# Reordering every engine's list of steps in a fused layer kernel, so that fp32r matmuls stand in fewer groups

## What is computed

```python
h = _L0_tok_ref(...)                    # S4D: K = 2 Re sum_n Cc[c,h,n] exp(dtA[h,n] * l), l < 1024
h = concat([cls_tok, h], axis=1)        # 129 rows of 64 steps
h = h + attn(layernorm(h))              # 1024 -> 128, gelu, two passes of one hydra block, 128 -> 1024
h = h + ffn(layernorm(h))               # 1024 -> 1024, plus a routed low-rank term of 8 experts

def hydra(u):                           # d 128, inner 256, 4 heads, state 16, conv of 7 taps
    z, xBC, dt = split(u @ in_w.T)
    dt = softplus(dt + dt_bias)         # forward and backward
    xs, B, C = split(silu(causal_conv(xBC)))
    y = scan forward + scan backward, shifted by one step, + xs * (xs @ fcD_w.T + D)
    yz = y * silu(z)
    return (yz * rsqrt(mean(yz**2) + 1e-5) * norm_w) @ out_w.T

def ffn(x):
    logits = x @ router_W.T + router_b  # 15; softmax, top 8, mapped to experts
    return x @ base_W.T + base_b + 2 * ((x @ A.T) * w) @ B
```

## Time and profile before

| | |
|---|---|
| median of 3 runs | 2334.94 us (2334.63 to 2346.7) |
| profiled execution | 2339.94 us, span 2338.2 us |
| PE busy | 2161.3 us, 92% of the span |
| DVE busy | 1847.3 us, 79% |
| ACT busy | 1528.2 us, 65% |
| POOL busy | 1091.2 us, 47% |
| mean granted clock | 0.968 |
| DMA | 132.61 MB, mean 57 GB/s |

### The profile page before, as it was taken

One profiled execution on the slowest core, in us unless ns is written; L12 is line 12 of the kernel. 1 busy time (PEld: TensorE's weight loads), 2 busy tenths in 40 slices (PEclk: granted clock), 3 DMA queues, 4 the chain that ended last, 5 costly groups with the idle time before them and its releaser, 6 DMA issues.

```text
span 2338.2 us, 51899 instructions
## 1 busy us (share of the span) xinstructions
PE 2161.3 (92%) x14117; PEld 1805.6 (77%) x14117; DVE 1847.3 (79%) x4980; ACT 1528.2 (65%) x2921; POOL 1091.2 (47%) x1350
## 2 busy tenths in 40 slices
PE   1356799999999999999999999999999999999998
PEld 1245688888888888888888888888888888888776
DVE  6847688888888888888888888888888888888764
ACT  2546576766677766667666767666777666676652
POOL 2534355444455444455444554444554444554331
PEclk9756799999999999999999999999999999999999
DMA  4400122112222122221122221122211222211211
GB/s 92 117 29 24 35 64 64 42 54 63 63 63 61 35 61 63 63 63 48 47 63 63 63 63 40 55 63 63 63 58 36 63 63 63 63 47 47 69 39 33
DMA packets 90061, 132.61 MB, mean 57 GB/s; under 512 B 20379, under 2 KB 63559, under 8 KB 90006
## 3 DMA queue, kind: packets, MB, share of 16 engines
q1 hardware_dynamic: 79176, 125.60, 18.2%
q10 hardware_dynamic: 10830, 6.35, 1.1%
HBM read 55.17 MB, written 76.74 MB: 56 GB/s over the span
## 4 chain that ended last, share of the span: by engine, by line
issue 43%; PE 27%; POOL 9%; DVE 7%; ACT 6%; POOLq 1%; DVEq 0%; ACTq 0%; DMA 0%; SPq 0%
PE bank L1611 5%; PE bank L1512 5%; POOL CB L901 4%; PE bank L1567 3%; PE bank L1542 2%; DVE NF L1241 2%; ACT L1006 2%; POOL XD L852 2%; PE bank L1685 1%; PE bank L1669 1%; POOL RS L886 1%; PE bank L1544 1%; PE bank L1543 1%; POOL RS L865 1%; PE bank L1659 1%
## 5 line engine op out<-in xcount | busy, mean ns | idle before, releaser
L1512 PE MATMUL bank<-w_hi,XHI 128*128 128x512 f32 (+1 forms) x1560 | 622.9, 399 | 0.0
L1512 PE MATMUL bank<-w_lo,XHI 128*128 128x512 f32 (+1 forms) x1560 | 554.7, 356 | 0.0
L1512 PE MATMUL bank<-w_hi,XLO 128*128 128x512 f32 (+1 forms) x1560 | 554.4, 355 | 0.0
L1147 DVE SCALAR_TENSOR_TENSOR CX<-bank,cw,CX 128x252 f32<-128x252 f32 (+5 forms) x804 | 335.7, 460 | 61.8 <-ACT CX L944 61.6
L901 POOL TENSOR_TENSOR CB<-CB,CM 48x252 f32<-48x252 f32 (+5 forms) x402 | 292.7, 728 | 153.6 <-ACT CM L929 142.7
L1512 PEld LDWEIGHTS bank<-w_hi,XLO 128*128 128x128 f32 x1560 | 295.5, 189 | 46.9
L1512 PEld LDWEIGHTS bank<-w_lo,XHI 128*128 128x128 f32 x1560 | 296.8, 190 | 41.4
L1512 PEld LDWEIGHTS bank<-w_hi,XHI 128*128 128x128 f32 x1560 | 296.4, 190 | 41.2
L929 ACT ACTIVATE T<-bank 64x512 f32<-64x512 f32 x256 | 151.4, 592 | 261.1 <-PE bank L1601 256.5
L865 POOL TENSOR_TENSOR RS<-VE,half_neg 128x1 f32<-128x1 f32 x65 | 35.5, 546 | 369.9 <-DVE VE L1339 369.9
L892 POOL TENSOR_TENSOR RB<-m_gt,AS 128x512 fp32r<-128x512 f32 x134 | 164.9, 1231 | 56.8 <-DVE AS L1413 56.8
(11 more groups left out here) (295 smaller groups left out, 5332.5 us busy)
## 6 DMA issues: line engine op xcount, KB each, us to landing
carried<-T SPq DMA_DIRECT2D x65, 512.0 KB, 4.8
T<-carried SPq DMA_DIRECT2D x65, 512.0 KB, 3.9
out<-HB SPq DMA_DIRECT2D x129, 256.0 KB, 3.2
tables<-tab SPq DMA_DIRECT2D x8, 560.0 KB, 4.3
TB<-tables SPq DMA_DIRECT2D x64, 70.0 KB, 2.7
carried<-U SPq DMA_DIRECT2D x65, 64.0 KB, 3.6
XM<-carried SPq DMA_DIRECT2D x65, 64.0 KB, 4.8
XI<-in_x SPq DMA_DIRECT2D x128, 32.0 KB, 2.8
```

Of the source, the lines that this page charges most:

```text
L1147: inc(STT(CX[:, c, :, s:CS], src[:, :, 0:CS - s], cw[:, c, k:k + 1], CX[:, c, :, s:CS], ALU.mult, ALU.add), "conv")
L1512: ins = mm(bank[:, 0:c1 - c0], xs_[:, 1 - p, k, :], ws[:, k, c0:c1], start=(c0 == HID and k == 0 and n == 0), stop=(last == k and n == 2))
```

## The change

Only the order of calls at the end of the `body` functions of POOL, ACT, DVE and PE. No step is added or taken away, no wait and no operand is changed, and SP's list is the same. The core of the diff (of DVE's list, 76 lines long, the two parts that are spoken of):

```diff
@@ GpSimd @@
+                    kernel_q()
                     swap()
-                    kernel_q()
...
                     add_bc(1)
+                    add_bc(2)
                     deviation_1()
-                    add_bc(2)
                     add_bc(3)
                     add_bc(4)
                     root_2()
+                    carry_h()
                     add_bc(5)
+                    add_bc(6)
                     decays_back(0)
-                    add_bc(6)
                     decays_back(1)
-                    carry_h()
@@ ScalarE @@
+                    exp_decays()
+                    keep_xs()
                     keep_x()
-                    keep_xs()
-                    exp_decays()
+                    squares(0)
+                    conv_first(0)
+                    conv_first(1)
+                    squares(1)
                     keep_h(0, 0)
                     keep_h(0, 1)
-                    squares(0)
-                    squares(1)
-                    conv_first(0)
-                    conv_first(1)
                     norm_y(0)
                     norm_y(1)
                     keep_h(1, 0)
+                    exp_router()
+                    keep_y()
                     keep_h(1, 1)
-                    keep_y()
-                    exp_router()
...
                     silu_x()
-                    split_hi(0)
                     silu_bc(0)
                     silu_bc(1)
+                    split_hi(0)
                     split_hi(1)
@@ VectorE @@
-                    kernel_p()
                     gram(0)
                     gram(1)
+                    kernel_p()
+                    gram_forth()
                     kernel_sum()
-                    gram_forth()
                     gram_sum()
-                    mix_matrix()
                     shift_real()
                     skip_scale()
+                    mix_matrix()
                     shift_sum()
                     add_skip()
                     times_z()
...
@@ TensorE @@
+                    turn_xs()
                     grams()
-                    turn_xs()
                     decay_sums()
                     turn_x()
+                    bases(1, 0, 1)
+                    route(0, 1)
+                    bases(1, 1, 2)
+                    bases(1, 2, 3)
                     bases(0, 0, 1)
-                    route(0, 1)
-                    bases(1, 0, 1)
-                    bases(1, 1, 2)
+                    bases(0, 1, 2)
                     route(1, 2)
-                    bases(0, 1, 2)
+                    mix()
+                    s4d(0)
+                    project_x()
                     route(2, 3)
                     route(3, 4)
-                    mix()
-                    s4d(0)
                     route(4, 5)
-                    project_x()
                     route(5, 6)
+                    route(6, 7)
+                    bases(0, 2, 3)
+                    route(7, 8)
                     s4d(1)
-                    route(6, 7)
-                    route(7, 8)
-                    bases(0, 2, 3)
+                    turn_y()
                     bases(0, 3, 4)
-                    turn_y()
                     bases(0, 4, 5)
-                    bases(1, 2, 3)
                     project_out()
                     bases(0, 5, 6)
                     project_bc()
                     up(0)
                     bases(1, 3, 4)
+                    bases(1, 4, 5)
+                    up(1)
                     bases(0, 6, 7)
-                    up(1)
+                    turn_h()
                     project_z()
-                    bases(1, 4, 5)
                     turn_a(0)
+                    bases(1, 5, 6)
+                    bases(1, 6, 7)
                     bases(0, 7, 8)
-                    bases(1, 5, 6)
-                    turn_h()
-                    bases(1, 6, 7)
+                    lora(0)
                     turn_a(1)
                     bases(1, 7, 8)
-                    lora(0)
                     lora(1)
                     turn_d(0)
                     down()
```

More of the change, by code:

```diff
@@ L1104, in body @@
                     scale_bc(1)
-                    exp_dt()
                     scale_bc(2)
                     scale_bc(3)
+                    exp_dt()
                     norm_1()
+                    keep_w()
                     scale_bc(4)
                     scale_bc(5)
+                    silu_z()
+                    keep_turned(0)
                     scale_bc(6)
-                    keep_turned(0)
-                    silu_z()
-                    keep_w()
                     norm_2()
@@ L1432, in body @@
                     times_z()
+                    conv(1, 0)
                     mean_square()
-                    conv(1, 0)
+                    gated_a()
                     conv(1, 1)
                     conv(2, 0)
+                    router(0)
                     conv(2, 1)
+                    router(1)
                     conv(3, 0)
                     conv(3, 1)
+                    conv(4, 0)
                     stats_1(0)
-                    gated_a()
-                    router(0)
+                    router(2)
@@ L1443, in body @@
+                    gated_b()
+                    layer_out()
                     stats_1(1)
-                    router(1)
-                    layer_out()
-                    gated_b()
+                    gated_lo()
+                    router(3)
                     stats_1(2)
[L1448 to L1454, removed]
@@ L1455, in body @@
                     router(4)
                     router(5)
+                    stats_1(3)
                     softplus(0)
+                    router(6)
+                    shift_1()
                     softplus(1)
+                    router(7)
                     residual(0)
-                    router(6)
+                    stats_2(0)
                     softplus(2)
-                    shift_1()
                     softplus(3)
-                    router(7)
-                    stats_2(0)
+                    router(8)
@@ L1466, in body @@
+                    conv(4, 1)
+                    softplus(4)
                     residual(1)
-                    softplus(4)
+                    conv(5, 0)
+                    softplus(5)
                     stats_2(1)
-                    softplus(5)
                     softplus(6)
-                    conv(5, 1)
                     stats_2(2)
                     softplus(7)
+                    weighted_lo()
+                    stats_2(3)
                     softplus(8)
-                    router(8)
@@ L1476, in body @@
                     softplus(9)
+                    conv(5, 1)
+                    shift_2()
                     softplus(10)
+                    conv(6, 0)
                     softplus(11)
-                    stats_2(3)
-                    conv(6, 0)
                     softplus(12)
-                    shift_2()
                     conv(6, 1)
                     split_decays(0)
-                    weighted_lo()
                     split_decays(1)
                     decays_forth(0)
+                    final(0)
@@ L1488, in body @@
+                    split_lo(0)
                     decays_forth(1)
-                    split_lo(0)
-                    final(0)
                     final(1)
```

## The result

| | |
|---|---|
| after | 2388.45 us, median of 4 runs (2385.41 to 2390.99) |
| before, on the same chip | 2339.95 us, median of 4 runs (2334.63 to 2346.7) |
| ratio | 1.0203, 95% interval 1.0171 to 1.0234: slower |
| span of the profiled execution | 2383.7 us (before 2338.2) |

The forecast was 2367, with a range of 2341 to 2388: the measured time lies at its upper end, and the loss beside the kernel before on the same chip is 48.5 us where 32 was forecast. The page of the changed kernel: first the span, then the busy time of each engine, then the granted clock in 40 slices.

The account below looks back on a forecast made before the run. PE was taken as the bound. Per iteration +0.55 at project_out, +0.03, -0.22 at lora(0), +0.20 at turn_d(1) and -0.04 for type changes gave +0.52 us; over 62, +32 us on 2334.9: 2367, range 2341 to 2388.

Parts of the forecast that it names:

- Bound and mechanism: PE bounds the kernel and meets new waits for other engines; an iteration lasts about 32.6 us.
- Changes of type, -0.04: Four fewer places on PE where fp32r follows fp32, at 0.01 us each: -0.04 us an iteration.
- `project_x`, 0.15: On PE, project_x now follows s4d(0) at once and waits 0.15 us for add_skip, starting at 9.76.
- one overlap fits: Argument that one DVE and POOL overlap ahead of s4d(0) delays nothing: shift_sum ends about 8.7, PE arrives at 8.74.
- rival C: DVE and POOL collide at shift_sum, everything from s4d(0) on is late by 0.4 us; chance 0.20.
- `s4d(1)`, 0.33 for the copies: PE waits 0.33 us at s4d(1) for ACT's two keep_h copies, now behind squares and conv_first; start at 13.77.
- C's sum (0.92, 2392): The 0.4 us lateness from s4d(0) on gives 0.92 us an iteration, +57 us, 2392; chance 0.20.
- `keep_y`, 0.19: On PE, project_out waits 0.19 us for ACT's keep_y, behind the late s4d(1) and exp_router.
- `project_bc`, `up(1)`, `lora(0)`: Later places on PE: nothing changes up to project_bc, up(1) costs 0.03 us, lora(0) loses its 0.22 us wait.
- `turn_d(1)`, 0.20: On PE, turn_d(1) waits 0.20 us because ACT's split_hi(0), now behind two silu_bc, makes split_lo(0) late.
- Count: The loss per iteration was multiplied by 62: 59 iterations with all parts, plus partial ones at the ends.

Follow-up runs that it names:

- e2: As e1, but the six fp32r matmuls of lora stand one by one between the eight fp32 matmuls of down; 2400.99 us, ratio 1.026.
- e5: The changed kernel with GpSimd's skip cut to half its columns in the loop; 2371.44 us, ratio 1.0112.
- e7: The changed kernel with ScalarE's two copies keep_h(0, 0) and keep_h(0, 1) back ahead of squares(0); 2434.27 us, ratio 1.0389.
- e9: The changed kernel with ScalarE's split_hi(0) back ahead of silu_bc(0) and silu_bc(1); 2362.68 us, ratio 1.0089.
- e12: The changed kernel with the edits of e5 and e9 together; 2345.6 us, ratio 1.002.
- e4: The kernel before with VectorE's weighted_lo moved ahead of conv(6, 1); 2340.31 us, ratio 1.0003.
- e6: The changed kernel with VectorE's mix_matrix back ahead of shift_real, as in the kernel before; 2389.39 us, ratio 1.0195.
- e10: The kernel before with about 40 steps moved in the four engine lists to take away each wait of TensorE; 2658.08 us, ratio 1.1357.
- e1: The kernel before with TensorE's turn_d(0) moved ahead of lora(0) and lora(1); 2402.58 us, ratio 1.0259.

## Why the forecast was right in kind and short in size

**Bound and mechanism.** Slower, since PE meets new waits for the other engines: right. The iteration took 32.76 us where 32.6 was said.

**Changes of type, -0.04.** Right: 1.10 and 1.11 us for the same group, and e2 gives 0.00.

**`project_x`, 0.15.** This step failed. It rested on `s4d(0)` being unmoved at 8.74; that start moved to 9.25, and `project_x` came at 10.19 instead of 9.76. The wait for `add_skip`, of which the 0.15 was made, is not there: `add_skip` is as early as before, and from `s4d(0)` to `project_x` are 0.94 us here and 0.95 in e5. In its place stand two overlaps one behind the other in nearly every iteration (56 waits), `shift_imag` with `shift_real` and `skip` with `shift_sum`; the forecast let one pass as harmless ("one overlap fits"), and the second is the one that rival C describes. e5 sizes it: 0.36. The Trainium skill (SBUF — State Buffer, "Who interferes with whom") says who issues first has the port for the whole instruction; by that rule, the trace agrees: `skip` starts 0.25 us ahead, and `shift_sum` takes 1.39 instead of 0.56, so it gets its turn about when `skip` ends (0.14 us before the end that the profile gives).

**`s4d(1)`, 0.33 for the copies.** The start was right (13.82 for 13.77), the reason only in part: the copies do end just 0.05 us ahead of it, but they are late because `conv_first` waits for `project_x`. And PE hardly waits for them: in e7, where they stand first, it needs 3.53 us from `project_x` to the second `s4d`, so here it is ready at 10.19 + 3.53 = 13.72, 0.10 ahead of 13.82. In e5, where `project_x` is at 9.77 as forecast, the second `s4d` follows 3.69 later, 0.05 behind the end of the copies: there the wait that the forecast described is real, and it is 0.16, half of the 0.33. The forecast had put this work at 0.87 + 2.10 + 0.71 = 3.68, too long, but started it at 9.76. So C's sum (0.92, 2392) was wrong as well: it put the late first `s4d` on top of a wait that is not there once `project_x` is late. Its 2392 comes near the 2388 only because the end of the iteration costs more than either had.

**`keep_y`, 0.19.** Not there: from `turn_y` to `project_out` are 1.83 us, before 1.84. With it out and 0.23 more at `turn_y`, 0.55 and the measured 0.58 meet by errors that cancel.

**`project_bc`, `up(1)`, `lora(0)`.** Forecast 0, 0.03 and -0.22; measured 0.07, 0.08 and -0.23 (from `up(1)` to `turn_d(0)`).

**`turn_d(1)`, 0.20.** Right in kind, too small: e9 gives 0.35. The forecast ended the chain at `turn_d(1)`; it goes on through `split_lo(1)` and DVE's list into the next iteration, where `mix` and the first `s4d` wait. Seen so, the loss is 0.35 (this) + 0.36 (`skip`) = 0.71 of 0.70, and the gain at `lora(0)` is used up by the small ones: in e12, with both causes away, `turn_y` is still 0.15 later than before and `up(1)` 0.29, and `turn_d(0)` only 0.05. What makes up these small ones was not tried one by one. Nor was `skip` cut in the kernel before; that it would gain nothing there is argued, from PE's waits for `add_skip` (1.6 us in 4 places in all).

**Count.** 45.5 us of span over 0.70 is 65 iterations, not 62. So most of the miss in size is the 0.18 us an iteration, 12 us, and not the count.

## What to carry to other kernels

With lists in a fixed order, price a move by what it does to the list of every engine that is nearly full, not only at the place where the bound engine waits: a wait removed at one place (e4, e6) came back whole at the next. Where VectorE's instructions read two operands from SBUF, lay its list beside GpSimd's and look for pairs that would start together, above all in the last steps before a matmul; the sign of such a pair is an instruction whose mean is twice its lone duration. And measure the cost that a change is meant to save before making it: here it was nothing.

## What was not expected of the hardware

**A queue of GpSimd instructions can hold VectorE for longer than one of them.** In e10 `decays_forth(1)` lasted 4.32 us. First the timeline of DVE in e10, then that of POOL:

```profile
1273.74 4.32 DVE L1401 TENSOR_TENSOR RF<-m_lt,AS 128x512 fp32r<-128x512 f32 x1
```

```profile
1273.26 2.04 POOL L892 TENSOR_TENSOR RB<-m_gt,AS 128x512 fp32r<-128x512 f32 x2
1275.30 1.19 POOL L880 TENSOR_SCALAR T<-T,SD,NM 128x1024 f32<-128x1024 f32 x1
1276.46 1.05 POOL L820 TENSOR_TENSOR V<-TB 128x512 f32<-128x512 f32 x1
1277.46 0.74 POOL L813 COPY XSW<-XI 128x128 f32<-128x128 f32 x1
```

Four instructions of POOL in a row, none of which is slowed (1.02 each for the first two), and DVE gets its turn only behind them: 1278.06 less the 0.69 of a free `decays_forth` is 1277.37. The fifth, the copy to XSW, takes 0.74 where it takes 0.29 alone, so there POOL is the one that waits. It is so in every iteration of the middle: `decays_forth(1)` lasts 4.32 to 4.33 in each. In other places (1.20 for `gram_sum`) DVE waited for one instruction only. What decides between the two was not tried.

**A wait of 3 us costs more than 3 us.** In e10, in windows around `turn_d(1)` (length, PE busy and instructions, granted clock, DMA share, GB/s):

```profile
1274.00:1278.00 4.00, 1.74 (x16) 1.00 0.00 0
1278.00:1280.00 2.00, 1.29 (x7) 0.76 0.00 0
1280.00:1282.00 2.00, 2.00 (x15) 0.50 0.65 131
...
1286.00:1290.00 4.00, 4.00 (x41) 1.00 0.21 71
```

After the wait of 2.98 us the granted clock goes from 1.00 to 0.50 (2.4 to 1.2 GHz) and stays there for about 6 us, so the iteration is 5.5 us longer than before (37.55 against 32.06), not 3. Not all of the other 2.4 us is the clock's: the first `s4d` waits 0.24 to 0.35 us in e10 as well. In e1, with a wait of 1.3 us in each iteration, the granted clock stays at 1.00 in the loop, and in the changed kernel, where waits of more than 0.4 us are rare, no slice from the sixth on is under 9 tenths but the last.
